# Attention's output bias: from an addition on GpSimd to a product with a row of ones on TensorE

## The chip, the cores and the metric

The kernel runs on one core of a Trainium2 chip. The metric is the device time of one execution in microseconds (us). Before the change its median is 1267.84 us over three runs (1267.67 to 1268.17).

## The reference

Two blocks of a small transformer, each an attention part and a mixture of experts, on x of 16 sequences x 256 tokens x 128 features, all in 32-bit floats. The change touches only the first part, attention with a selection of 32 keys for each query:

```python
# x is the layer norm of the residual rows here
Q, K, V = split(x @ w_qkv.T + b_qkv)            # Q and K are rotated (rope)
iq = (x @ w_iq.T + b_iq).reshape(B, S, 4, 64)   # index queries, 4 heads of 64
ik = x @ w_ik.T + b_ik
iw = x @ w_iw.T + b_iw                          # one weight for each index head
head_scores  = relu(einsum('bqhd,bkd->bhqk', iq, ik))
index_scores = einsum('bhqk,bqh->bqk', head_scores, iw)
# the 32 keys of highest index score stay, all others get -inf
attn = softmax(Q @ K.T / sqrt(128) + mask)
return (attn @ V) @ w_o.T + b_o                 # b_o: 128 numbers; added to the residual x
```

Since each row of `attn` sums to one, `attn @ (V @ w_o.T + ones * b_o)` is the same result as `(attn @ V) @ w_o.T + b_o`.

Behind it come a routed mixture of experts (8 experts, 2 for each token), a state-space part and a second mixture of experts. None of their code changes.

## The kernel before

The program is written by hand for each engine: TensorE (PE in the rows), VectorE (DVE), ScalarE (ACT), GpSimd (POOL) and SyncE (SP, it starts transfers). Each engine runs its own list in order, and semaphores order the engines. There is no planner; the order of work is the order in the source.

**Attention** (`attention`, lines 144 to 534) is a software pipeline over 16 sequences ("batches", s = 0 to 15), in 18 steps. In step s three batches are under work: the `front` of batch s, the `middle` of batch s - 1 and the `tail` of batch s - 2. Within a step each engine does, in this order:

- TensorE: transposes the normalised rows of batch s (L238, it waits for `iw_copied` of batch s - 1, which VectorE gives at L408); the products for Q and K (L245), index queries (L254), and index keys and V (L257); the logits of batch s - 1 (L269, it waits for `qk_sum`, GpSimd's rotated Q and K); V times w_o and the index weights of batch s (L276, L279), which it signals by `vo_ready`; the index scores of the first half of the queries (L296), the transposes of the probabilities of batch s - 2 (L304), the index scores of the second half (L296), and the product of probabilities and V times w_o (L316).
- ScalarE: copies the transposed rows (L343), exponentials of batch s - 2 (L347), copies with biases (L357, L361, L365), the copy of V times w_o into `VO` once `vo_ready` has come (L371), the normalised rows of batch s + 1 (L330), relu of the index scores, first half (L380), the copy of the transposed probabilities (L389), relu of the second half (L382, L383).
- VectorE: in step s it weights and adds the index scores of batch s - 1 (L419 for the first head, it waits for `relu_ready`; L422 for the other three), finds the 32 largest in four rounds of eight (L434, L438), updates the residual rows of batch s - 3 (L454, L460), takes the index weights of batch s out of PSUM (L408, it waits for `vo_copied`), and masks the logits of batch s - 1 (L442, L447, L450).
- GpSimd: adds the output bias to the residual rows of batch s (L517), multiplies Q and K by the rope table (L520, it waits for `rope_parts`, L357), adds the two parts (L525).

Some steps carry work of the next part, the dispatch of tokens to experts, beside this: a square root on ScalarE in steps 8 and 10 (L679) for which VectorE waits (L685), transposes and router products on TensorE in steps 10 and 11 (L716, L735), the choice of experts on VectorE in step 12, and from step 12 on four indirect DMAs for each step on GpSimd (L846) and scaling of the residual rows on ScalarE (L832). When all engines are through with attention, a barrier ends it. Then GpSimd issues the other 12 indirect DMAs of the first half of the tokens, and when these have landed, SyncE fetches the first tile of rows for the experts, which TensorE transposes at L1129.

The product of the change's line, before:

```python
for t in range(2):
    nc.tensor.matmul(b0[:, t * D:(t + 1) * D], IKV[v][:, S + t * P:S + (t + 1) * P],
                     w[:, 8 * P + IH:9 * P + IH], start=True, stop=True)
```

Each such product of 32-bit floats shows as two matmuls and two weight loads in the trace.

Of the kernel before, what the change touches and what calls it, by code (L numbers as in the profile page):

```python
# [12 lines left out]
ALU = mybir.AluOpType  # L13
# [3 lines left out]
B, S, D = 16, 256, 128  # L17
P = 128
T = B * S // P
TOPK = 32  # L20
IH, ID = 4, 64
# [8 lines left out]
ds = bass.ds  # L30
# [113 lines left out]
def attention(nc, rows, early, d, zeroed, X, shift, scales, ident, w, bias, b_iw, b_o, rope, loads, clear):  # L144
# [3 lines left out]
    with ExitStack() as ctx:  # L148
        m = Maker(nc, ctx, "at_")
        W2 = 2 * P  # L150
# [21 lines left out]
        b0, b12a, b12b, b3, b4 = bank  # L172
# [6 lines left out]
        xn_ready = m.sig("xn_ready", 2)  # L179
# [25 lines left out]
        x_updated = m.sig("x_updated", 2)  # L205


        b_added = m.sig("b_added")

        def steps(eng, step):  # L210

            step(0, 0, True, False, False)
            step(1, 1, True, True, False)
            for s in range(2, B):
                step(s, s % 4, True, True, True)
            step(B, 0, False, True, True)
            step(B + 1, 1, False, False, True)
# [4 lines left out]
        with nc.Block() as block:  # L222
            @block.sync
            def _(sp):
                loads(sp)

            @block.tensor
            def _(pe):
                def step(s, q, front, middle, tail):
# [42 lines left out]
                    if front:  # L272

                        pe.wait_ge(ikv_copied.sem, ikv_copied.after(s))
                        for t in range(2):
                            nc.tensor.matmul(b0[:, t * D:(t + 1) * D], IKV[v][:, S + t * P:S + (t + 1) * P],  # L276
                                             w[:, 8 * P + IH:9 * P + IH], start=True, stop=True)
                        for t in range(2):
                            ins = nc.tensor.matmul(b0[:, W2 + t * IH:W2 + (t + 1) * IH], xT[v][:, t * P:(t + 1) * P],  # L279
                                                   w[:, 8 * P:8 * P + IH], start=True, stop=True)  # L280
                        ins.then_inc(vo_ready.sem, 1)
                        pe.wait_ge(iq_copied.sem, iq_copied.after(s))
# [36 lines left out]
                    if s in TURN:  # L319
                        d.tensor_score(pe, TURN[s])  # L320

                steps(pe, step)

            @block.scalar
# [79 lines left out]
            def _(dve):  # L404
# [47 lines left out]
                def update(s, v):  # L452
                    dve.wait_ge(probs_ready.sem, probs_ready.after(s))
                    nc.vector.reciprocal(rinv[v][:], rsum[v][:]).then_inc(rinv_ready.sem, 1)  # L454
                    dve.wait_ge(rinv_ready.sem, rinv_ready.after(s))
                    dve.wait_ge(av_ready.sem, av_ready.after(s))
                    dve.wait_ge(b_added.sem, b_added.after(s))
                    for t in range(2):
                        x = X[:, ds(s * W2 + t * D, D)]
                        nc.vector.scalar_tensor_tensor(x, b4[:, t * D:(t + 1) * D], rinv[v][:, t:t + 1], x,  # L460
                                                       ALU.mult, ALU.add).then_inc(x_updated.sem, 1)
# [41 lines left out]

            @block.gpsimd
            def _(pool):
                clear()

                def step(s, q, front, middle, tail):
                    v = q % 2
                    if front:  # L510


                        pool.wait_ge(xn_ready.sem, xn_ready.after(s))
                        if s >= LAST:
                            pool.wait_ge(idx.sem, idx.after(s - 1))
                        x = X[:, ds(s * W2, W2)].rearrange("p (t d) -> p t d", d=D)
                        nc.gpsimd.tensor_tensor(x, x, b_o[:].unsqueeze(1).to_broadcast([P, 2, D]), ALU.add).then_inc(b_added.sem, 1)  # L517
                        pool.wait_ge(rope_parts.sem, rope_parts.after(s))
                        parts = RP[v][:].rearrange("p (r k s) -> p r k s", r=2, k=2)
                        nc.gpsimd.tensor_tensor(parts, parts, rope[:].rearrange("p (r s) -> p r s", r=2).unsqueeze(2).to_broadcast([P, 2, 2, S]),  # L520
                                                ALU.mult).then_inc(rotated.sem, 1)
                        pool.wait_ge(rotated.sem, rotated.after(s))
                        if not (isinstance(s, int) and s < 2):
                            pool.wait_ge(logits_ready.sem, logits_ready.after(s - 2))
                        nc.gpsimd.tensor_tensor(QK[v][:], RP[v][:, 0:2 * S], RP[v][:, 2 * S:4 * S], ALU.add).then_inc(qk_sum.sem, 1)  # L525
                    if s == LAST:
                        pool.wait_ge(zeroed.sem, zeroed.after(1))
                        d.pool_reweight(pool, 0, 0)
                    if LAST <= s < LAST + 4:
                        d.pool_scatter(pool, 0, HT // 4 * (s - LAST), HT // 4 * (s - LAST + 1), ALU.add)  # L530

                steps(pool, step)
                d.pool_reweight(pool, 0, 1)
                d.pool_scatter(pool, 1, 0, HT // 4, ALU.add)
# [1588 lines left out]
```

## Time and profile before

| | |
|---|---|
| median of three runs | 1267.84 us (1267.67 to 1268.17) |
| the profiled execution | 1262.61 us, its span 1260.8 us |
| TensorE busy / its weight loads | 989.4 us (78%) / 599.9 us (48%) |
| VectorE busy | 942.6 us (75%) |
| GpSimd busy | 837.2 us (66%) |
| ScalarE busy | 736.0 us (58%) |
| attention, from the start to its last instruction on VectorE | 232.46 us |

The span is the time between the first and the last instruction of the profiled execution; what lies around it is 1.8 us. All positions are in us from the start of the span. Shares of busy time are means over parts that different engines bound, so the argument is made from the attention part alone. In a timeline row the first number is the start, the second the time from the first to the end of the last of the merged instructions ("x4": four of them), then come engine, line, operation and output<-input; in brackets stands how long the engine had been idle before and who released it.

### The profile page before, as it was taken

The numbers are of one execution on the slowest core, as the hardware profiler recorded it, in microseconds if no ns is written. First come the engines' busy times: TensorE is split into PE (matmuls) and PEld (weight loads), VectorE is DVE, ScalarE is ACT, GpSimd is POOL, SyncE is SP. The second block draws the span as 40 slices with busy tenths as digits, with TensorE's granted clock in tenths as the row PEclk, the third lists the DMA queues.
The fourth block names the chain that finished last, engine by engine and source line by source line (L and its number), as shares of the span: only waits on it lengthen the run. The fifth ranks groups of instructions, "written<-read, shape, count | busy, mean of one in ns | idle before, by whom it ended". The sixth has DMA issues, their size and how long they took to land. (4 is left out here: it accounts for less than half of the span.)

```text
span 1260.8 us, 17033 instructions
## 1 busy us (share of the span) xinstructions
PE 989.4 (78%) x4202; PEld 599.9 (48%) x4202; DVE 942.6 (75%) x2310; ACT 736.0 (58%) x1636; POOL 837.2 (66%) x604
## 2 busy tenths in 40 slices
PE   5888867469999977888888888888876324989990
PEld 4666755348888832323242424333221223757770
DVE  6999899553333438899998989999998852757781
ACT  4767747255555568776666766867542213768750
POOL 3334248647437455989898987788966077747876
PEclk9998889579999989899989998989989656989995
DMA  9993012336535424444444443435442014746553
GB/s 272 177 162 129 1 10 22 30 49 93 82 68 94 81 41 122 132 145 136 144 135 141 138 146 127 137 133 169 146 149 89 1 46 76 121 88 123 114 103 65
DMA packets 140480, 133.50 MB, mean 106 GB/s; under 512 B 14578, under 2 KB 121698, under 8 KB 140258
## 3 DMA queue, kind: packets, MB, share of 16 engines
q1 hardware_dynamic: 107106, 115.55, 33.8%
q0 software_dynamic: 33280, 16.86, 11.9%
q8 instruction: 39, 0.64, 0.2%
q14 instruction: 55, 0.45, 0.1%
HBM read 98.66 MB, written 31.60 MB: 103 GB/s over the span
## 5 line engine op out<-in xcount | busy, mean ns | idle before, releaser
L1855 POOL TENSOR_TENSOR ss_HC<-ss_Hs,ss_Cb 128x512 f32<-128x512 f32 x256 | 325.2, 1367 | 83.0 <-PE ss_Y L1605 66.1
L1605 PE MATMUL ss_Y<-ss_HC,g_ident 128*128 128x512 f32 x512 | 270.9, 648 | 48.6 <-POOL ss_HC L1855 42.0
L1899 DVE TENSOR_TENSOR_SCAN ss_Hs<-ss_dA,ss_dBu 128x512 f32<-128x512 f32 x256 | 296.7, 1199 | 7.5 <-ACT ss_dA L1765 7.5
L846 POOL DMA_INDIRECT rows<-m_XS,g_slot x128 | 181.2, 1416 | 67.9 <-issue 35.8
L1765 ACT ACTIVATE ss_dA<-ss_delta,g_A 128x510 f32<-128x510 f32 x256 | 168.4, 712 | 74.2 <-DVE ss_Hs L1899 74.0
L1138 PE MATMUL m_x_UP<-g_m_w,m_x_gT 128*128 (+1 forms) x532 | 193.2, 469 | 0.0
L1605 PEld LDWEIGHTS ss_Y<-ss_HC,g_ident 128*128 128x128 f32 x512 | 92.1, 200 | 211.7 <-POOL ss_HC L1855 155.5
L1891 DVE TENSOR_TENSOR ss_dBu<-ss_duP,ss_Bb 128x512 f32<-128x512 f32 x256 | 162.8, 681 | 10.7 <-DMA ss_Bb<-bc_rows 9.1
L1158 PEld LDWEIGHTS m_x_DP<-g_m_w,m_x_hT 128*128 128x128 f32 x908 | 122.8, 191 | 61.7 <-issue 35.6
L1158 PE MATMUL m_x_DP<-g_m_w,m_x_hT 128*128 (+1 forms) x908 | 140.9, 285 | 2.4 <-ACT m_x_hT L1230 2.3
L1279 DVE SCALAR_TENSOR_TENSOR m_x_hid<-m_x_UP,m_x_G,m_x_sg 128x352 f32<-128x352 f32 x78 | 45.5, 583 | 116.4 <-ACT m_x_sg L1212 108.9
L1230 ACT ACTIVATE m_x_hT<-m_x_HP 128x256 f32<-128x256 f32 (+1 forms) x188 | 80.3, 427 | 87.1 <-PE m_x_HP L1148 55.4
L1118 POOL DMA_INDIRECT g_X<-out_rows,g_slot x64 | 99.6, 1557 | 37.9 <-issue 18.3
L520 POOL TENSOR_TENSOR at_RP<-at_RP,a_rope 128x1024 f32<-128x1024 f32 x16 | 39.6, 2475 | 90.9 <-ACT at_RP L357 90.9
L1138 PEld LDWEIGHTS m_x_UP<-g_m_w,m_x_gT 128*128 128x128 f32 x532 | 88.0, 194 | 18.1 <-issue 1.6
L1129 PE MATMUL m_x_TP<-g_ident,m_x_G 128*128 128x128 f32 x188 | 52.6, 280 | 38.4 <-DMA m_x_G<-rows 37.2
L1148 PE MATMUL m_x_HP<-g_ident,m_x_hid 128*128 128x128 f32 x454 | 80.6, 273 | 2.5 <-DVE m_x_hid L1279 2.5
L1286 DVE TENSOR_TENSOR m_x_sg<-m_x_UP,g_m_b 128x352 f32<-128x352 f32 x110 | 57.6, 524 | 33.0 <-PE m_x_UP L1138 24.7
L1106 POOL DMA_INDIRECT g_X<-out_rows,g_slot x32 | 49.3, 1540 | 44.3 <-DMA out_rows<-m_x_YO 32.8
L1570 PE MATMUL ss_Q<-ss_xpad,ss_w_conv 128*128 128x512 f32 x128 | 58.9, 605 | 5.8 <-ACT ss_xpad L1695 5.8
L1212 ACT ACTIVATE m_x_sg<-m_x_UP 128x352 f32<-128x352 f32 x78 | 36.2, 464 | 38.7 <-PE m_x_UP L1138 37.6
L1148 PEld LDWEIGHTS m_x_HP<-g_ident,m_x_hid 128*128 128x128 f32 x454 | 56.1, 142 | 4.0 <-DVE m_x_hid L1279 2.6
(271 smaller groups left out, 1746.7 us busy)
## 6 DMA issues: line engine op xcount, KB each, us to landing
ss_Bb<-bc_rows SPq DMA_DIRECT2D x64, 512.0 KB, 4.9
ss_Cb<-bc_rows SPq DMA_DIRECT2D x64, 512.0 KB
rows<-g_Z SPq DMA_DIRECT2D x2, 5031.0 KB, 49.1
m_x_G<-rows SPq DMA_DIRECT2D x156, 64.5 KB
out_rows<-m_x_YO SPq DMA_DIRECT2D x156, 64.0 KB
g_m_w<-in_w_up SPq DMA_DIRECT2D x1, 2816.0 KB, 10.7
g_m_b<-in_b SPq DMA_DIRECT2D x1, 2160.0 KB, 11.7
g_X<-in_x SPq DMA_DIRECT2D x4, 512.0 KB, 6.1
```

What stands on the lines that cost most here:

```text
L846: self.nc.gpsimd.indirect_dma_start(self.XG, bass.IndirectOffsetOnAxis(self.rt.slot[k][:, t:t + 1], 0), self.XS[:, t, :], None, compute_op ...
L1118: nc.gpsimd.indirect_dma_start(X[:, t * D:(t + 1) * D], None, Y[0:(h + 1) * NH * P, :], bass.IndirectOffsetOnAxis(rt.slot[k][:, t:t + 1], ...
L1138: ins = nc.tensor.matmul(UP[v % 2][:, at:at + n], gT[v % 2][:], w.w[:, ds(e + c, n)], start=True, stop=True)
L1148: ins = nc.tensor.transpose(HP[0:n, c * P:(c + 1) * P], hid[v % 2][:, c0:c0 + n], ident[:])
L1158: ins = nc.tensor.matmul(DP[v % 2][:, 0:D], hT[v % 2][0:n, c * P:(c + 1) * P], w.w[0:n, ds(e + WU + c * D, D)], start=c == 0, stop=c == NC ...
L1230: ins = nc.scalar.activation(hT[v % 2][:, 0:full], HP[:, 0:full], ACT.Copy)
L1570: ins = nc.tensor.matmul(dst, w_conv[:, h, k, :], xpad[:, h, :, k:k + S], start=k == 0, stop=k == K)
L1605: ins = nc.tensor.matmul(Yp[:, h, :], ident[:], HC[n % 2][:, h, :], start=False, stop=n == N - 1)
L1765: nc.scalar.activation(dA[n % NA][:, h, :, 1:S], seqs(delta[v][:, h, :])[:, :, 1:S], ACT.Exp, scale=A[:, h, n:n + 1]).then_inc(dA_ready.se ...
L1855: nc.gpsimd.tensor_tensor(HC[n % 2][:, h, :], Hs[n % 4][:, h, :], Cb[g % 2][:, n % 2, :], ALU.mult).then_inc(hc_ready.sem, 1)
L1891: v_.tensor_tensor(dBu[:, h, :], duP[:, h, :], Bb[g % 2][:, n % 2, :], ALU.mult).then_inc(dBu_ready.sem, 1)
L1899: v_.tensor_tensor_scan(Hs[n % 4][:, h, :], dA[n % NA][:, h, :, :].rearrange("p s t -> p (s t)"), dBu[:, h, :], 0.0, ALU.mult, ALU.add).th ...
```

## The change

The residual rows no longer get the bias from GpSimd. Instead TensorE adds it to the rows of V times w_o, as a product of a row of 128 ones (one partition high) with `b_o` (its first partition), accumulated into the same PSUM region. VectorE no longer waits for `b_added` in its update, and GpSimd no longer waits for the normalised rows. A memset of the row of ones on GpSimd is new, with a wait for it on TensorE in step 0.

```diff
-        b_added = m.sig("b_added")
+        row, row_set = m.sb("row", [1, P]), m.sem("row_set")
...
                         pe.wait_ge(ikv_copied.sem, ikv_copied.after(s))
+                        if s == 0:
+                            pe.wait_ge(row_set, 1)
                         for t in range(2):
                             nc.tensor.matmul(b0[:, t * D:(t + 1) * D], IKV[v][:, S + t * P:S + (t + 1) * P],
-                                             w[:, 8 * P + IH:9 * P + IH], start=True, stop=True)
+                                             w[:, 8 * P + IH:9 * P + IH], start=True, stop=False)
+                            nc.tensor.matmul(b0[:, t * D:(t + 1) * D], row[0:1, :], b_o[0:1, :], start=False, stop=True)
...
                     dve.wait_ge(av_ready.sem, av_ready.after(s))
-                    dve.wait_ge(b_added.sem, b_added.after(s))
...
             def _(pool):
+                nc.gpsimd.memset(row[:], 1.0).then_inc(row_set, 1)
                 clear()
...
-                        pool.wait_ge(xn_ready.sem, xn_ready.after(s))
                         if s >= LAST:
                             pool.wait_ge(idx.sem, idx.after(s - 1))
-                        x = X[:, ds(s * W2, W2)].rearrange("p (t d) -> p t d", d=D)
-                        nc.gpsimd.tensor_tensor(x, x, b_o[:].unsqueeze(1).to_broadcast([P, 2, D]), ALU.add).then_inc(b_added.sem, 1)
```

## Rows read from the trace of the kernel before

**Rows 1.** Busy time by stretch: span, PE, PEld, DVE, ACT, POOL, PEclk, DMA, GB/s

```profile
54.00:66.00 12.00, 11.00 (x70) 8.59 (x66) 11.90 (x50) 9.35 (x23) 4.36 (x3) 1.00 1.27 185
...
92.00:94.00 2.00, 2.00 (x6) 1.53 (x6) 2.00 (x7) 0.37 (x2) 0.00 (x0) 0.50 0.83 203
...
290.00:310.00 20.00, 20.00 (x123) 16.19 (x122) 6.58 (x18) 10.78 (x27) 14.75 (x12) 1.00 0.59 92
```

**Rows 2.** Groups of POOL, 0 to 235: busy, mean ns | idle before, releasers

```profile
L520 POOL TENSOR_TENSOR at_RP<-at_RP,a_rope 128x1024 f32<-128x1024 f32 x16 | 39.6, 2475 | 90.9 <-ACT at_RP L357 90.9
...
L517 POOL TENSOR_TENSOR g_X<-g_X,a_b_o 128x256 f32<-128x256 f32 x16 | 13.4, 835 | 7.1 <-DVE at_WK L422 5.7 <-ACT at_Xn L330 0.8
```

**Rows 3.** Timeline, TensorE around the changed product, step 15

```profile
210.79 0.52 PEld L276 LDWEIGHTS at_b<-a_w,at_IKV 128*128 128x128 f32 x4 [0.93 <-ACT at_IKV L365]
...
211.23 0.53 PEld L279 LDWEIGHTS at_b<-a_w,at_xT 128*128 128x128 f32 x4
...
211.77 1.13 PE L296 MATMUL at_SC<-at_IKV,at_IQ 64*128 64x256 f32 x8
```

**Rows 4.** Timeline, one round between ScalarE and TensorE, step 15

```profile
203.24 0.59 ACT L383 ACTIVATE at_R<-at_b 128x512 f32<-128x512 f32 x1
...
205.26 0.37 ACT L343 ACTIVATE at_xT<-at_b 128x256 f32<-128x256 f32 x1
...
205.68 1.99 PE L245 MATMUL at_b<-at_xT,a_w 128*128 128x256 f32 x8 [1.64 <-ACT at_xT L343]
...
211.88 0.38 ACT L371 ACTIVATE at_VO<-at_b 128x256 f32<-128x256 f32 x1 [1.14 <-PE at_b L279]
...
215.10 0.59 ACT L383 ACTIVATE at_R<-at_b 128x512 f32<-128x512 f32 x1
```

**Rows 5.** Timeline, the instructions before which VectorE waited for ScalarE

```profile
23.70 0.35 DVE L419 TENSOR_SCALAR at_WK<-at_R,at_IW 128x256 f32<-128x256 f32 x1 [0.55 <-ACT at_R L383]
...
112.22 0.25 DVE L685 RECIPROCAL m_d_sc<-m_d_t 128x16 f32<-128x16 f32 x1 [0.41 <-ACT m_d_t L679]
...
128.28 0.35 DVE L419 TENSOR_SCALAR at_WK<-at_R,at_IW 128x256 f32<-128x256 f32 x1 [1.28 <-ACT at_R L383]
...
140.06 0.25 DVE L685 RECIPROCAL m_d_sc<-m_d_t 128x16 f32<-128x16 f32 x1 [1.03 <-ACT m_d_t L679]
...
157.30 0.35 DVE L419 TENSOR_SCALAR at_WK<-at_R,at_IW 128x256 f32<-128x256 f32 x1 [1.21 <-ACT at_R L383]
```

**Rows 6.** Timeline, first weighting of batch 15 on VectorE

```profile
215.56 0.62 DVE L419 TENSOR_SCALAR at_WK<-at_R,at_IW 128x256 f32<-128x256 f32 x2
```

**Rows 7.** Timeline, first product of steps 3, 6 and 7 on TensorE

```profile
44.62 0.38 PE L238 MATMUL at_b<-g_ident,at_Xn 128*128 128x128 f32 x2
...
77.50 0.41 PE L238 MATMUL at_b<-g_ident,at_Xn 128*128 128x128 f32 x2 [0.36 <-DVE at_IW L408]
...
89.56 0.41 PE L238 MATMUL at_b<-g_ident,at_Xn 128*128 128x128 f32 x2 [1.18 <-DVE at_IW L408]
```

**Rows 8.** Timeline, VectorE's mask of steps 8, 14 and 15, GpSimd beside the last

```profile
100.61 0.43 DVE L442 TENSOR_SCALAR at_WK<-at_WK 128x512 f32<-128x512 f32 x1
...
201.64 1.09 DVE L442 TENSOR_SCALAR at_WK<-at_WK 128x512 f32<-128x512 f32 x1
...
213.08 1.27 POOL L525 TENSOR_TENSOR at_QK<-at_RP 128x512 f32<-128x512 f32 x1
213.16 1.48 DVE L442 TENSOR_SCALAR at_WK<-at_WK 128x512 f32<-128x512 f32 x1
```

**Rows 9.** Timeline, the Q and K products of steps 7 and 9

```profile
90.44 3.15 PE L245 MATMUL at_b<-at_xT,a_w 128*128 128x256 f32 x8 [0.47 <-ACT at_xT L343]
...
115.66 3.78 PE L245 MATMUL at_b<-at_xT,a_w 128*128 128x256 f32 x8 [1.37 <-ACT at_xT L343]
```

**Rows 10.** Timeline, end of attention and first expert tile

```profile
231.85 0.61 DVE L460 SCALAR_TENSOR_TENSOR g_X<-at_b,at_rinv,g_X 128x128 f32<-128x128 f32 x2 [3.83 <-PE at_b L316]
...
260.70 0.45 PE L1129 MATMUL m_x_TP<-g_ident,m_x_G 128*128 128x128 f32 x1 [8.65 <-DMA m_x_G<-rows]
```

## The prediction

> **What bounds the kernel now.** I read the busy time by stretch first. Inside attention VectorE is busy for 11.90 us of 12 in a plain stretch, and behind attention TensorE is busy for 20.00 of 20 while the expert tiles run [rows 1]. So the attention part has one length, set mostly by VectorE, and whatever moves its end moves all that follows: VectorE's last update at 231.85 lets the barrier go, GpSimd then issues its other twelve indirect DMAs, and the first expert tile at 260.70 has waited 8.65 us for rows that these bring [rows 10]. I take the shift of attention's end at full price for the whole time.
>
> Next I read who waits for whom up to 235 us. GpSimd's groups show that it is not the bound: before the rope product it idles for 90.9 us in total, waiting for ScalarE, and the bias addition that the change removes sits in front of that wait [rows 2]. What the reader is to look for instead is every place where VectorE waits for ScalarE, because there VectorE is not the bound and the round between TensorE and ScalarE is. There are five of weight: 0.55 us at 23.70, 0.41 at 112.22, 1.28 at 128.28, 1.03 at 140.06 and 1.21 at 157.30 [rows 5].
>
> Last I followed that round in a timeline. In step 15 it goes from the relu at 203.24 over the copy of transposed rows at 205.26, the Q and K products at 205.68 (TensorE had waited 1.64 us for that copy), further copies and products, the copy of V times w_o at 211.88, for which ScalarE waited 1.14 us on TensorE, to the next relu at 215.10: 11.86 us a round [rows 4]. The changed product lies on this round, between a copy that TensorE waited for (0.93 us) and a copy that ScalarE waits for [rows 3, 4]. Time put in there is not covered by either engine.
>
> **The change part by part.**
>
> *GpSimd loses 16 additions*, 13.4 us of its busy time at 0.835 us each [rows 2]. In steps 0 to 12 they only lengthen its wait for the rope parts: worth nothing. In steps 13 to 15 GpSimd has DMAs to issue and gets through earlier, by about 0.7 us for each step at most. Nobody waits for it at a signal there, but it shares something with VectorE: the mask takes 1.09 us at 201.64 and 1.48 us at 213.16, where GpSimd's addition from 213.08 to 214.35 runs beside it [rows 8]. The same instruction takes 0.43 us at 100.61, where GpSimd computes nothing beside it [rows 8]. So up to 0.66 + 1.05 = 1.7 us of VectorE's time can come back. I book it at nothing, because VectorE then only arrives earlier at the weighting of batches 14 and 15, and there it is barely behind ScalarE: the relu of batch 15 ends at 215.10 + 0.59 = 215.69, and of the two L419 instructions, 0.62 us together with one at 0.35, the second starts 0.27 us after the first, at 215.83 in batch 15 [rows 4 to 6]. That leaves 0.14 us (0.10 in batch 14, in the same way). If the round had room, the 1.7 us would be a gain; that is the lower bound of this part.
>
> The page GPSIMD Engine Reference of the Trainium skill, section Key points, says that GpSimd shares its SBUF interfaces with VectorE and contends with instructions in a two-port mode; the rows on the mask bear it out, and by that rule alone the change would gain the 1.7 us just named.
>
> *The wait for `b_added`* on VectorE and *the wait for the normalised rows* on GpSimd go: no idle time is laid to either in the list of waits, so nothing. *The memset of the row of ones* is one short instruction in front of three others on GpSimd, at 10.7 us, 9 us before TensorE needs it. It delays SyncE's weight transfers by as much, some 0.1 us (my estimate; the 128 x 256 addition that goes takes 0.835 us [rows 2]); the experts need these weights only after 130 us. Nothing. No DMA is added or moved.
>
> *TensorE gains* two products in each step, which show as four matmuls and four weight loads, since the product beside them does. Four of L276's take 0.44 us from start to the next line's start (210.79 to 211.23); four of L279's, with only 4 columns to stream, take 0.54 us (211.23 to 211.77) [rows 3]. The new ones have the shape of L276's apart from their height of one partition. No row shows that height. The nearest with fewer rows are the index scores on half the array: eight of 256 columns in 1.13 us [rows 3], against 1.99 us for eight of 256 columns on the full array [rows 4], about half. So the bounds for one step are 0.22 us (half of 0.44) and 0.54 us. I take d = 0.44 us: the gain of the half-height products comes from pairs that lie on different halves of the array, and here all four lie on the same partition.
>
> The Trainium skill's page TensorE: Matmul & The Clock Gate, section Why this matters for your kernels, states that a single product with 32 rows takes as long as one with 128. By that rule d is 0.44 us, by the half-height row 0.22; no run here shows which.
>
> *How d adds up on the end of attention.* I carry the lateness of TensorE's start of each step, with d = 0.44.
> - Batch 0: VectorE waits for the relu at 23.70 [rows 5], so VectorE is late by 0.44.
> - Step 2 starts when VectorE lets it (0.44). Step 3 starts at 44.62 without a wait, on TensorE's own time [rows 7]: 0.88; steps 4 and 5 likewise: 1.32, 1.76. Step 6 had waited 0.36: 1.76 + 0.44 - 0.36 = 1.84. Step 7 had waited 1.18: 1.84 + 0.44 - 1.18 = 1.10 [rows 7]. Step 8: 1.54. Whether VectorE feels it in batches 2 to 7 doesn't matter, since a wait there would be part of what is booked next.
> - Step 8, where VectorE waits for the root at 112.22: 1.54 + 0.44 = 1.98 late. The same at 128.28: 2.42; at 140.06: 2.86; at 157.30: 3.30 [rows 5].
> - Step 12 is long on VectorE alone, so the lateness stays 3.30. Batches 13, 14 and 15 run at the pace of the round: 3 x 0.44 = 1.32, less the 0.14 us of room in batch 15 [rows 4, 6]. Together 4.48 us.
>
> One thing in this sum is open: TensorE's clock. At 90.44 and 115.66 the eight Q and K products take 3.15 and 3.78 us [rows 9] against 1.99 [rows 4]; the granted clock is at 0.50 of full speed (1.2 GHz in place of 2.4) from 92 to 94, after TensorE had idled 1.18 and then 0.47 us in step 7 [rows 1, 7, 9]. With the lateness of 1.84 us the pause of 1.18 goes away. If the clock then holds, step 7 is shorter by 3.15 - 1.99 = 1.16 us and more in the next products, the lateness carried into step 8 is eaten, and only VectorE's own 0.44 stays: 0.44 + 6 x 0.44 - 0.14 = 2.94 us. No row tells which of the two comes; I take the middle, 3.7 us.
>
> **Sum.** The profiled execution took 1262.61 us, its span 1260.8 and 1.8 us around it, 5.2 us under the median of the runs, so a re-run of the same kernel can differ by as much as the sum that I make. Profiled: 1262.6 + 3.7 = 1266.3. Applied to the median: 1267.84 + 3.7 = **1271.5 us**. What a measurement can tell from no change is about 0.2%, 2.5 us.
>
> With d = 0.22 and the clock held: 0.22 + 6 x 0.22 - 0.14 = 1.4 us; with d = 0.54 and the clock as before: lateness 2.78 us in batch 8, then 6 x 0.54 - 0.14, 5.9 us. The likeliest case reaches from 1269.2 to 1273.7.
>
> **The rivals.**
> - *Hidden under VectorE (no change, 1267.8 us).* VectorE is busy 99% in plain steps [rows 1]. If the new products overlap with their neighbours, or the recovered 1.7 us of the masks [rows 8] balances a small d (d = 0.22 costs 1.4 us), nothing is left. Against it: VectorE's five waits, all on the round.
> - *The clock holds where it fell before (faster, 1264.7 us).* More work on TensorE could keep the granted clock up in steps 7, 9, 11 and 12. In step 9 that alone is 3.78 - 1.99 = 1.8 us on the Q and K products [rows 4, 9]. It can give VectorE no more than its waits, 1.28 + 1.03 + 1.21 = 3.5 us [rows 5], less 0.44 for batch 0: 3.1 us. It decides once step 9 runs at full clock, since it gains more than four times d. Against it: the fall at 115.66 comes after a wait of 1.37 us that depends on a table load of ScalarE and VectorE's scales, and the change leaves both. The Trainium skill's page TensorE: Matmul & The Clock Gate, section What's actually happening, says that the clock goes by how busy TensorE has been of late; the profile agrees so far that the low stretches come behind idle ones.
> - *The clock falls in more places (slower, 1275.1 us).* The shifted steps put the pauses of steps 14 to 16 elsewhere. In step 15 TensorE waits 1.64 us before the Q and K products and still has the full clock for them [rows 4], after a pause as long as the two of step 7 together. One fall costs 1.8 us in these products as at 115.66 [rows 4, 9], and about as much again in the products behind (my estimate, at the same ratio of 3.78 to 1.99): 3.6 us on top of 3.7.
> - *The change does not do what it says:* excluded by the diff; both products of a step run, the addition is gone.
>
> **How the numbers follow.** The round lengthened: 0.52. Hidden: 0.18. Clock held, faster: 0.13. Clock falls more: 0.17. Slower by over 0.2% (above 1270.4) is 0.17 and some 0.44 of the first case: 0.61. Within 0.2%: 0.18 + 0.08 = 0.26. Faster: 0.13. The range reaches from 1266 us, a part of the gain by the clock, to 1276 us, one further fall.
>
> **What would show it.** Right: the L276 line with twice as many instructions, L279 starting 0.9 us behind L276's start instead of 0.44; ScalarE's wait at L371 at 1.6 us instead of 1.14; VectorE's waits at L419 and L685 longer, new ones at batches 14 and 15; the mask at 0.4 to 0.6 us in steps 14 and 15; VectorE's last L460 2.9 to 4.5 us later than 231.85, and the first tile later by the same. Wrong: L371's wait longer by less than 0.3 us (d), an attention end that has not moved although the waits grew (cover that I missed), Q and K products at 1.99 us in steps 7 and 9 or at over 3 us elsewhere (the clock), or a difference that arises behind 260 us.

## The result: slower by 1.5%, five times the predicted loss

| kernel | median, us | lowest to highest | runs |
|---|---|---|---|
| before | 1267.76 | 1266.86 to 1268.17 | 4 |
| changed | 1286.20 | 1283.62 to 1287.28 | 4 |

The ratio is 1.0146, 95% interval 1.0132 to 1.0161: 18.4 us more, where 3.7 were predicted and 1276 us was the top of the range. The direction was right, the size was not. The profiled execution of the changed kernel took 1286.36 us, at its median; that of before took 1262.61 us, 5.2 below its own, so the two traces lie 23.7 us apart (spans 1284.5 and 1260.8) and some 5 of these are luck of that one execution of before.

Nearly all of it arises in attention. VectorE's last update starts 23.3 us later than at 231.85 [rows 10], the first expert tile 21.6 us later, with less waiting in front of it; the last 2.1 us between the two spans arise behind that tile. The timeline of the changed kernel:

```profile
255.17 0.61 DVE L462 SCALAR_TENSOR_TENSOR g_X<-at_b,at_rinv,g_X 128x128 f32<-128x128 f32 x2 [3.84 <-PE at_b L319]
...
282.30 0.45 PE L1129 MATMUL m_x_TP<-g_ident,m_x_G 128*128 128x128 f32 x1 [5.57 <-DMA m_x_G<-rows]
```

The changed product, step 4, TensorE's timeline (start, us, engine, line, operation; "x2" is one product, since each shows as two matmuls). In this kernel V's product is L278, the bias product L280, the index weights L282, the scores L299:

```profile
57.02 0.49 PE L278 MATMUL at_b<-a_w,at_IKV 128*128 128x128 f32 x2 [0.53 <-ACT at_IKV L368]
57.44 0.48 PE L280 MATMUL at_b<-a_b_o,at_row 1*128 1x128 f32 x2
57.85 0.49 PE L278 MATMUL at_b<-a_w,at_IKV 128*128 128x128 f32 x2
58.27 0.48 PE L280 MATMUL at_b<-a_b_o,at_row 1*128 1x128 f32 x2
58.68 0.61 PE L282 MATMUL at_b<-a_w,at_xT 128*128 128x4 f32 x4
59.22 1.55 PE L299 MATMUL at_SC<-at_IKV,at_IQ 64*128 64x256 f32 x8
60.70 1.11 PE L307 MATMUL at_b<-g_ident,at_PR 128*128 128x128 f32 x4
61.75 1.84 PE L299 MATMUL at_b<-at_IKV,at_IQ 64*128 64x256 f32 x8
```

The same place in the kernel before (there L276 is V's product, L279 the index weights, L296 the scores):

```profile
61.28 0.71 PE L276 MATMUL at_b<-a_w,at_IKV 128*128 128x128 f32 x4 [0.53 <-ACT at_IKV L365]
61.83 0.51 PE L279 MATMUL at_b<-a_w,at_xT 128*128 128x4 f32 x4
62.26 1.13 PE L296 MATMUL at_SC<-at_IKV,at_IQ 64*128 64x256 f32 x8
63.33 0.66 PE L304 MATMUL at_b<-g_ident,at_PR 128*128 128x128 f32 x4
63.91 1.13 PE L296 MATMUL at_b<-at_IKV,at_IQ 64*128 64x256 f32 x8
```

Read the starts, not the durations. From V's first product to the scores it was 62.26 - 61.28 = 0.98 us and is 59.22 - 57.02 = 2.20. So d, the price of the two bias products in one step, is 1.22 us, where I took 0.44 and bounded it at 0.54. The second thing to see is behind the group: the second scores take 1.84 us where they took 1.13. The granted clock says why (busy time by stretch; the third figure from the end is TensorE's granted clock as a share of 2.4 GHz):

```profile
50.00:52.00 2.00, 1.53 (x13) 1.24 (x11) 0.71 (x3) 1.62 (x4) 0.00 (x0) 1.00 1.28 148
...
60.00:62.00 2.00, 2.00 (x10) 1.02 (x10) 1.97 (x10) 1.64 (x4) 0.00 (x0) 0.50 1.26 186
62.00:64.00 2.00, 2.00 (x12) 1.42 (x13) 0.59 (x4) 0.82 (x2) 0.00 (x0) 0.70 1.24 164
```

It is at 1.2 GHz for a while in each of steps 2 to 5, where before it stood at 1.00 up to 90 us. In the stretch from 54 to 66 VectorE is busy for 9.76 us of 12, against 11.90 [rows 1]:

```profile
54.00:66.00 12.00, 11.00 (x57) 7.97 (x56) 9.76 (x42) 7.89 (x19) 3.62 (x2) 0.86 1.27 181
```

and its list of waits up to 245 us (total, times, longest) lays 23 waits of VectorE for ScalarE, 30.7 us together, to the four lines below. The same lines of the kernel before have 9 waits and 7.2 us in that list; [rows 5] shows the five that the prediction built on:

```profile
DVE at_WK L422 <- ACT at_R L386: 18.8, 12, 2.3
...
DVE m_d_sc L685 <- ACT m_d_t L679: 4.4, 2, 2.2
DVE at_WK L422 <- ACT at_R L383: 4.2, 5, 1.7
DVE at_IW L411 <- ACT at_VO L374: 3.3, 4, 1.8
```

### The profile page after: what moved, and what is told of

Read it like the earlier page. It is cut to its first block and busy times, and to the rows that moved or that the text cites. A ratio compares the mean times of both kernels' runs of the same rounds, so it can differ in the third digit from the quotient of the medians.

```text
span 1284.5 us, 17147 instructions
## 1 busy us (share of the span) xinstructions
PE 1019.8 (79%) x4266; PEld 618.0 (48%) x4266; DVE 943.1 (73%) x2310; ACT 736.0 (57%) x1636; POOL 824.8 (64%) x589
## 3 DMA queue, kind: packets, MB, share of 16 engines
q0 software_dynamic: 33280, 16.86, 11.7%
## 5 line engine op out<-in xcount | busy, mean ns | idle before, releaser
L1118 POOL DMA_INDIRECT g_X<-out_rows,g_slot x64 | 100.2, 1566 | 37.7 <-issue 18.6
## 6 DMA issues: line engine op xcount, KB each, us to landing
g_m_b<-in_b SPq DMA_DIRECT2D x1, 2160.0 KB, 11.4
```

The costliest lines, as they stand in the source:

```text
L1118: nc.gpsimd.indirect_dma_start(X[:, t * D:(t + 1) * D], None, Y[0:(h + 1) * NH * P, :], bass.IndirectOffsetOnAxis(rt.slot[k][:, t:t + 1], ...
```

## The experiments

Two theories stood after the result. **A**: what costs is the change of height. Between a product of 128 rows and one of 1 row lie 0.42 us from start to start, between two of 128 rows 0.22; four such changes in a step. **B**: the added products cost as such, or the half of the change on GpSimd does something that I didn't see (the rivals R1 to R3 of the expectations are forms of it). Below, "round" is the time from TensorE's logits product to that of the next step (steps 4 to 5 unless said), and d is taken as above, from V's first product to the scores. The kernels of one batch ran on one chip beside the kernel before, whose medians there were 1267.59, 1266.63 and 1266.63 us, with more scatter than in the first measurement (1260.39 to 1272.46 us in the first batch). Each ratio is the estimate of its batch with its 95% interval, and can differ by 0.2% from the ratio of two medians. A trace shows one execution: those of the grouped kernel, of the one product and of the 64 and 32 rows are the fastest of their four, that of the changed kernel's repetition is the slowest of its four.

**No bias at all.** GpSimd's addition is gone and nothing is in its place, so the bias is left out of the result.

```diff
-        b_added = m.sig("b_added")
...
-                    dve.wait_ge(b_added.sem, b_added.after(s))
...
-                        pool.wait_ge(xn_ready.sem, xn_ready.after(s))
...
-                        x = X[:, ds(s * W2, W2)].rearrange("p (t d) -> p t d", d=D)
-                        nc.gpsimd.tensor_tensor(x, x, b_o[:].unsqueeze(1).to_broadcast([P, 2, D]), ALU.add).then_inc(b_added.sem, 1)
```

> The GpSimd half of the change alone: its addition goes and no product comes in its place (the output bias is left out). Theory A, the loss of 18.4 us lies in TensorE's product alone: 1266 to 1268 us, with the masks of steps 14 and 15 near 0.43 us where they took 1.09 and 1.48 us. Rival R1, part of the loss comes from taking work off GpSimd (its operations now start elsewhere beside VectorE): above 1270 us.

Measured 1263.18 us, ratio 0.9976 (0.9943 to 1.0008): below the 1266 to 1268 us expected, and within the noise the time of before. The masks of steps 14 and 15 take 0.43 us, as expected, and attention ends only 0.3 us earlier (231.54 against 231.85). GpSimd's half of the change is worth nothing that can be measured, and costs nothing.

**The product alone.** The product of height 1 is added and GpSimd's addition kept; the bias is counted twice.

```diff
+        b_added.base = 1
+        row = m.sb("row", [1, P])
...
+                        if s == 0:
+                            pe.wait_ge(b_added.sem, 1)
...
-                                             w[:, 8 * P + IH:9 * P + IH], start=True, stop=True)
+                                             w[:, 8 * P + IH:9 * P + IH], start=True, stop=False)
+                            nc.tensor.matmul(b0[:, t * D:(t + 1) * D], row[0:1, :], b_o[0:1, :], start=False, stop=True)
...
+                nc.gpsimd.memset(row[:], 1.0).then_inc(b_added.sem, 1)
```

> The TensorE half alone: the product of height one is added and GpSimd keeps its addition (the output bias is counted twice). Theory A: as the changed kernel, 1283 to 1288 us, with 1.66 us from the first V product to the index weights' product where before it was 0.55. Rival R1: clearly below 1280 us.

Measured 1286.3 us, ratio 1.016 (1.0096 to 1.0225), the whole loss; d is 1.22 us here too. It is TensorE's half alone.

**Full height.** The stationary operand is 128 x 128 with 1/128 everywhere, and all 128 equal rows of the bias stream through: the same sum, and no change of height.

```diff
-        row, row_set = m.sb("row", [1, P]), m.sem("row_set")
+        row, row_set = m.sb("row", [P, P]), m.sem("row_set")
...
-                            nc.tensor.matmul(b0[:, t * D:(t + 1) * D], row[0:1, :], b_o[0:1, :], start=False, stop=True)
+                            nc.tensor.matmul(b0[:, t * D:(t + 1) * D], row[:], b_o[:], start=False, stop=True)
...
-                nc.gpsimd.memset(row[:], 1.0).then_inc(row_set, 1)
+                nc.gpsimd.memset(row[:], 1.0 / P).then_inc(row_set, 1)
```

> Same number and width of products, but 128 partitions high (128 x 128 of 1/128, times all 128 equal rows of b_o). Theory A, the price is the change of height between 128 and 1, some 0.2 us at each of four changes in a step: now d falls from 1.2 to the forecast 0.44 us, the clock no longer falls in steps 2 to 5, and the time is 1270 to 1273 us, what the prediction's sum gave. Rival R2, four more matmuls of any shape cost this much (the round was fuller than read): 1280 us or more.

Measured 1264.19 us, ratio 0.9993 (0.997 to 1.0015), faster than the 1270 to 1273 us expected. TensorE's timeline:

```profile
62.46 0.49 PE L278 MATMUL at_b<-a_w,at_IKV 128*128 128x128 f32 x2 [0.53 <-ACT at_IKV L368]
62.78 0.39 PE L280 MATMUL at_b<-a_b_o,at_row 128*128 128x128 f32 x2
63.01 0.39 PE L278 MATMUL at_b<-a_w,at_IKV 128*128 128x128 f32 x2
63.23 0.39 PE L280 MATMUL at_b<-a_b_o,at_row 128*128 128x128 f32 x2
63.45 0.51 PE L282 MATMUL at_b<-a_w,at_xT 128*128 128x4 f32 x4
63.89 1.13 PE L299 MATMUL at_SC<-at_IKV,at_IQ 64*128 64x256 f32 x8
```

128 times the arithmetic, the same number of products accumulated into the same region, and the loss is gone: 0.22 us from product to product, d = 63.89 - 62.46 - 0.98 = 0.45 us. The weight loads show what differs. Here the loads for the bias product start 0.11 us ahead of its matmul (62.67 against 62.78):

```profile
62.45 0.30 PEld L278 LDWEIGHTS at_b<-a_w,at_IKV 128*128 128x128 f32 x2 [0.93 <-ACT at_IKV L368]
62.67 0.30 PEld L280 LDWEIGHTS at_b<-a_b_o,at_row 128*128 128x128 f32 x2
```

In the changed kernel they don't run ahead (57.43 against 57.44):

```profile
57.02 0.30 PEld L278 LDWEIGHTS at_b<-a_w,at_IKV 128*128 128x128 f32 x2 [0.93 <-ACT at_IKV L368]
57.43 0.29 PEld L280 LDWEIGHTS at_b<-a_b_o,at_row 1*128 1x128 f32 x2
```

**Grouped: two changes of height in place of four.** First both products of V, then both of height 1.

```diff
                         for t in range(2):
                             nc.tensor.matmul(b0[:, t * D:(t + 1) * D], IKV[v][:, S + t * P:S + (t + 1) * P],
-                                             w[:, 8 * P + IH:9 * P + IH], start=True, stop=False)
-                            nc.tensor.matmul(b0[:, t * D:(t + 1) * D], row[0:1, :], b_o[0:1, :], start=False, stop=True)
+                                             w[:, 8 * P + IH:9 * P + IH], start=t == 0, stop=False)
+                        for t in range(2):
+                            nc.tensor.matmul(b0[:, t * D:(t + 1) * D], row[0:1, :], b_o[0:1, :], start=False, stop=t == 1)
```

> Height one, but both V products first and then both bias products, so two changes of height in a step and not four. Theory A: d = 4 x 0.11 + 2 x 0.2 = 0.84 us, and a time between the full-height kernel and the changed one, about 1276 to 1281 us. Rival R3, each product of height one is slow in itself, wherever it stands: as the changed kernel, 1283 us or more.

Measured 1281.02 us, ratio 1.0124 (1.0071 to 1.0178). Its four runs, 1275.12 to 1285.60 us, don't tell it from the changed kernel; the timeline does:

```profile
52.48 0.71 PE L278 MATMUL at_b<-a_w,at_IKV 128*128 128x128 f32 x4 [0.53 <-ACT at_IKV L369]
53.12 0.71 PE L281 MATMUL at_b<-a_b_o,at_row 1*128 1x128 f32 x4
53.76 0.61 PE L283 MATMUL at_b<-a_w,at_xT 128*128 128x4 f32 x4
54.30 1.13 PE L300 MATMUL at_SC<-at_IKV,at_IQ 64*128 64x256 f32 x8
```

d = 54.30 - 52.48 - 0.98 = 0.84 us. Against full height 0.39 us for two changes, 0.2 us each, as for the four of the changed kernel: (1.22 - 0.45) / 4 = 0.19.

**One product of height 1.** As grouped, but one product of 256 columns for both halves.

```diff
...
-                            nc.tensor.matmul(b0[:, t * D:(t + 1) * D], row[0:1, :], b_o[0:1, :], start=False, stop=True)
+                        nc.tensor.matmul(b0[:, 0:W2].rearrange("p (t d) -> p t d", d=D), row[0:1, :],
+                                         b_o[0:1, :].unsqueeze(1).to_broadcast([1, 2, D]), start=False, stop=True)
```

> The two products of V come first, and then one product of height 1 over both halves (256 columns) brings the bias: one change of height from 128 to 1 and one back, as in the grouped form, with one product of height 1 fewer. Theory A (each change of height between 128 and 1 costs about 0.2 us, whatever the number of products): the stretch from the first V product to the index weights is as in the grouped form, about 1.2 to 1.3 us, and the time about 1281 us, ratio 1.010 to 1.013. Theory B (each product of height 1 costs by itself): less than the grouped form by one product, and the time near 1275 us, ratio 1.006.

Measured 1281.23 us, ratio 1.0135 (1.009 to 1.0181); d = 0.82 us. Halving the number of products, at the same columns, changes nothing: two changes cost what they cost. Theory B's stretch, one product shorter than the grouped one, is out, and its 1275 us lies under each of the four runs (1276.42 to 1284.31).

**64 and 32 rows.** Is it height 1, or any height but 128? The ones are 1/64 on 64 partitions, then 1/32 on 32.

```diff
-        row, row_set = m.sb("row", [1, P]), m.sem("row_set")
+        row, row_set = m.sb("row", [64, P]), m.sem("row_set")
...
-                            nc.tensor.matmul(b0[:, t * D:(t + 1) * D], row[0:1, :], b_o[0:1, :], start=False, stop=True)
+                            nc.tensor.matmul(b0[:, t * D:(t + 1) * D], row[:], b_o[0:64, :], start=False, stop=True)
...
-                nc.gpsimd.memset(row[:], 1.0).then_inc(row_set, 1)
+                nc.gpsimd.memset(row[:], 1.0 / 64).then_inc(row_set, 1)
```

> The product of the change with 64 rows (a stationary operand of 1/64 on 64 partitions, 64 rows of the bias) where the change has 1 row; same order, same number of products. Theory A in its narrow form (height 1 is what costs): as with 128 rows, four products in 0.44 us more, time about 1264 to 1267 us, ratio 0.999 to 1.002. Theory A in its wide form (every change of height costs about 0.2 us): the stretch is 1.66 us as in the change, time 1283 to 1287 us, ratio 1.013 to 1.016. The index scores of height 64 follow products of height 128 in the kernel before with no gap of that size, so I expect the narrow form, or something between.

> The product of the change with 32 rows (stationary 1/32 on 32 partitions). Half height took exactly the stretch of height 1 (1.66 us from the first V product to the index weights) and lengthened the round from 10.69 to 11.91 us. Theory A in its wide form (every change of height costs about 0.2 us, whatever the height): again 1.66 us, rounds of 11.91 us where the clock is full, time 1279 to 1287 us, ratio 1.011 to 1.016. Theory C (the cost grows with the rows that are left out, and the agreement of 64 and 1 rows is an accident): another stretch than 1.66 us.

Measured for 64 rows 1281.56 us, ratio 1.014 (1.0092 to 1.0189), for 32 rows 1284.61 us, 1.0154 (1.0102 to 1.0205). I had leaned to the narrow form, and it was wrong. TensorE's timeline with 64 rows:

```profile
54.40 0.49 PE L278 MATMUL at_b<-a_w,at_IKV 128*128 128x128 f32 x2 [0.53 <-ACT at_IKV L368]
54.81 0.49 PE L280 MATMUL at_b<-a_b_o,at_row 64*128 64x128 f32 x2
55.23 0.49 PE L278 MATMUL at_b<-a_w,at_IKV 128*128 128x128 f32 x2
55.65 0.48 PE L280 MATMUL at_b<-a_b_o,at_row 64*128 64x128 f32 x2
56.06 0.61 PE L282 MATMUL at_b<-a_w,at_xT 128*128 128x4 f32 x4
56.60 1.13 PE L299 MATMUL at_SC<-at_IKV,at_IQ 64*128 64x256 f32 x8
```

The spacing is that of height 1 to 0.01 us, and with 32 rows too; d is 1.22 us for 64, 32 and 1 rows. Going from 128 rows to fewer and back is what costs, however many are left out. The scores behind the group take 1.13 us here: this execution has the lengthened stretch without the falls of the clock in steps 2 to 5.

**A change of height in TensorE's wait.** The kernel before, GpSimd's addition kept, with one more product per step, its result unread, issued where TensorE waits for the copies of IKV; once with 1 row, once with 128.

```diff
+                        pe.wait_ge(iq_copied.sem, iq_copied.after(s))
+                        nc.tensor.matmul(b3[:, 0:D], ident[0:1, :], b_o[0:1, :], start=True, stop=True)
                         pe.wait_ge(ikv_copied.sem, ikv_copied.after(s))
```

> The kernel before, GpSimd's addition kept, with one more product of height 1 in each step, whose result nobody reads: TensorE issues it after the logits, in its wait for the copies of IKV (0.53 us of idle time), so the two changes of height (about 0.3 us each) lie in that wait as far as it reaches. Theory A1 (the changes of height cost TensorE only the time in which nothing runs, and that time on the path is what is lost): V's products start at most 0.1 us later, the time is that of before within 2 us, ratio 0.999 to 1.002. Theory A2 (products of height 1 bring the granted clock down wherever they stand): the clock falls in steps 2 to 5 as in the changed kernel, although the round is hardly longer, and the time is 5 us or more above that of before.

> As the one with the product of height 1 in the wait, but with a product of 128 rows in its place: the difference between the two is that of height alone. Under each theory the time is that of before within 2 us (ratio 0.999 to 1.002) and the clock stays at 1.00 in steps 2 to 5; a time above that would say that an extra product in this place costs by itself, and then the one with the height 1 has to be read against this one.

Measured 1266.67 us, ratio 1.0007 (0.998 to 1.0033) with 1 row, and 1267.15 us, 1.0011 (0.9988 to 1.0034) with 128. The timeline of the first:

```profile
60.73 0.48 PE L275 MATMUL at_b<-a_b_o,g_ident 1*128 1x128 f32 x2
61.32 0.71 PE L278 MATMUL at_b<-a_w,at_IKV 128*128 128x128 f32 x4
...
62.30 1.14 PE L298 MATMUL at_SC<-at_IKV,at_IQ 64*128 64x256 f32 x8
```

V's product starts at 61.32, against 61.28 before. Two changes of height a step are free where TensorE would have idled, and the clock stays at 1.00 from 22 to 106 us. So in this execution products of low height didn't bring the clock down. The bias products themselves weren't put there: they write to the PSUM bank from which ScalarE is then still copying IKV, and no run shows what that would do.

This execution answers one more question. The clock did not fall in steps 7 and 9, where it falls before: the rounds that end there took 12.07 and 13.49 us against 13.74 and 16.33, and TensorE was 3.5 us ahead of before in step 9 (118.77 against 122.25). Step 12, which is long on VectorE, took it back; attention ended 0.3 us earlier.

**The same length without a change of height.** Three products of full height, each with a third of the bias, for each half.

```diff
-        row, row_set = m.sb("row", [1, P]), m.sem("row_set")
+        row, row_set = m.sb("row", [P, P]), m.sem("row_set")
...
-                            nc.tensor.matmul(b0[:, t * D:(t + 1) * D], row[0:1, :], b_o[0:1, :], start=False, stop=True)
+                            for k in range(3):
+                                nc.tensor.matmul(b0[:, t * D:(t + 1) * D], row[:], b_o[:], start=False, stop=k == 2)
...
-                nc.gpsimd.memset(row[:], 1.0).then_inc(row_set, 1)
+                nc.gpsimd.memset(row[:], 1.0 / (3 * P)).then_inc(row_set, 1)
```

> The bias as three products of height 128 for each half of V, each with a third of it (stationary 1/384): no change of height, but six products of 0.22 us, so the stretch from the first V product to the index weights should be 0.44 + 6 x 0.22 = 1.76 us, 0.1 us more than in the changed kernel. Theory D (only the length of the stretch counts: a round is 10.69 us plus what the stretch is longer by): rounds of 12.0 us in steps 3 to 5 where the clock is full, end of attention 16 to 18 us later than before, time 1280 to 1288 us, ratio 1.012 to 1.018. Theory A with a part of its own for the change of height beyond the stretch (the granted clock that falls in steps 2 to 5 of the changed kernel): no such falls here, rounds of 12.0 us all the same, time nearer 1278 to 1283 us, as with half height.

Measured 1277.73 us, ratio 1.0097 (1.0064 to 1.0129); d = 67.85 - 65.52 - 0.98 = 1.35 us. The round came out as foreseen, to 0.04 us:

```profile
51.92 1.03 PE L269 MATMUL at_LG<-at_QK 128*128 128x256 f32 x4
63.96 1.03 PE L269 MATMUL at_LG<-at_QK 128*128 128x256 f32 x4
76.00 1.03 PE L269 MATMUL at_LG<-at_QK 128*128 128x256 f32 x4
```

12.04 us a round, and no fall of the clock from 46 to 106 us. With a longer stretch than the changed kernel's it loses less than that kernel did in its own measurement (1.0132 to 1.0161), but the changed kernel repeated on this chip, below, gave 1.012 with an interval that overlaps. So length alone brings most of the loss: 0.97%, against 1.46% in the first measurement and 1.2% on this chip, with intervals too wide for a share. Theory D's 1280 to 1288 us was too high for it, and theory A's 1278 to 1283 us just so. Whether the rest belongs to the changes of height, beyond the time that they take, isn't shown.

**The changed kernel once more**, beside the last two.

> The changed kernel once more, on the chip of these runs, for a second profiled execution. If the granted clock falls in steps 2 to 5 belong to the change of height, rounds of 13.4 us are seen again in steps 2 to 5 and the attention ends 23 us later than before. If they differ from execution to execution, the rounds without a fall are of 11.91 us as with half height, and the end of attention lies anywhere from 16 us (no falls) to 23 us (four more falls) later; the time is then 1279 to 1287 us, ratio 1.012 to 1.016.

Measured 1281.97 us, ratio 1.012 (1.0072 to 1.0167). Its attention ends 23.2 us later than before, as in the first execution, but by another way. Round by round, TensorE's logits products of the first execution:

```profile
41.80 1.03 PE L269 MATMUL at_LG<-at_QK 128*128 128x256 f32 x4
55.46 1.03 PE L269 MATMUL at_LG<-at_QK 128*128 128x256 f32 x4
68.92 1.03 PE L269 MATMUL at_LG<-at_QK 128*128 128x256 f32 x4
82.38 1.03 PE L269 MATMUL at_LG<-at_QK 128*128 128x256 f32 x4
```

13.66, 13.46, 13.46 us. In the second: 13.61, then 11.91, 11.90, 11.91 us; it had lost 6.6 us already by step 1, in stretches at the lower clock:

```profile
22.00:26.00 4.00, 4.00 (x19) 3.39 (x20) 0.17 (x1) 1.62 (x4) 0.47 (x1) 0.56 1.14 329
26.00:30.00 4.00, 3.05 (x11) 1.74 (x10) 2.01 (x6) 2.01 (x5) 0.00 (x0) 0.50 1.22 254
```

So the second expectation holds: the falls are not in the same steps each time, the rounds without one are of 11.91 us, and that both executions end 23 us late lies at the end of what it allowed.

All profiled executions side by side. "Late" is the start of TensorE's logits product in that step, and of VectorE's last update, against the execution of before, in us; the last column is my prediction's own sum, 14 d - 1.68 with the clock as before. "Late" holds a difference of the start as well: V's first product, before any bias product has run, starts between 19.14 us (changed) and 20.79 (changed, again), at 20.51 with 64 and 20.29 with 32 rows, against 19.50 before.

| kernel | d | full-clock round | late, step 1 | step 8 | step 13 | last update | 14 d - 1.68 |
|---|---|---|---|---|---|---|---|
| before | 0 | 10.70 | 0 | 0 | 0 | 0 | |
| full height | 0.45 | 11.14 | 0.3 | -0.3 | 0.7 | 1.7 | 4.6 |
| one product of height 1 | 0.82 | 11.52 | 0.9 | 5.5 | 9.4 | 13.0 | 9.8 |
| grouped | 0.84 | 11.52 | 1.1 | 4.2 | 7.4 | 11.1 | 10.1 |
| 32 rows | 1.22 | 11.92 | 2.0 | 6.2 | 11.3 | 15.9 | 15.4 |
| 64 rows | 1.22 | 11.91 | 2.2 | 6.5 | 11.7 | 16.5 | 15.4 |
| product alone | 1.22 | 11.91 | 5.8 | 11.4 | 17.9 | 22.4 | 15.4 |
| changed, again | 1.22 | 11.91 | 6.6 | 12.1 | 18.6 | 23.2 | 15.4 |
| changed | 1.22 | 11.91 | 3.3 | 13.7 | 18.8 | 23.3 | 15.4 |
| longer, full height | 1.35 | 12.04 | 1.1 | 6.2 | 8.8 | 12.3 | 17.2 |

The third column is the cleanest reading of the study. For before it is the shortest of its rounds at full clock, in steps 2 to 6; the others go up to 11.24 us, with TensorE waiting for VectorE in step 6 [rows 7]. With the products a round takes 10.70 us plus d, to 0.02 us, in nine executions, in the rounds from step 3 to step 6 without a fall of the clock (in the changed kernel's first execution, from step 6 to step 8). So d is covered only as far as the rounds before were the longer ones, by up to 0.5 us: from step 2 to step 6 about half of it with full height (1.0 us more for four times 0.45), a fifth at d = 1.22 (64 rows: 4.1 us more for four times 1.22).

## Why the prediction was wrong, step by step

**The step that failed is the price of the two products, d.** "Four of L276's take 0.44 us [...] The new ones have the shape of L276's apart from their height of one partition. No row shows that height." I bounded d by 0.22 and 0.54 us; it was 1.22. By my own sum those 0.78 us more in each step are 10.9 of the 14.7 us that I was short. Both bounds came from products among their like, and neither contains what the change really adds, four switches between 128 rows and another height at 0.19 us each. I had set only the height against a row and not the order in which heights follow each other. The 0.44 itself was right for products of full height (0.45). The hint stood in the trace of before and I didn't look: the four matmuls of L304 lie between two groups of 64 rows and take 63.91 - 63.33 = 0.58 us from start to start, where four of L276's, the same shape among their like, took 0.44 [rows 3]; that is 0.14 us more. It is only the part of two switches that falls on this group. Matmul by matmul the scores on either side are stretched too: from the first pair of the second scores to the next pair it is 0.32 us, between the pairs behind 0.22, and as much is added on the other side. Together that is 0.35 us for two switches, 0.18 each. Four of them on top of 0.44 would have given 1.14 us and, by my own sum, 14.3 us of loss.

The upper bound of 0.54 held a part of a switch, and I read it as the price of four narrow products. The starts in [rows 3] are those of weight loads. The loads of L279 begin ahead of their matmul (211.23 against 211.34); those of the scores, with 64 rows, begin with theirs:

```profile
211.34 0.51 PE L279 MATMUL at_b<-a_w,at_xT 128*128 128x4 f32 x4
...
211.77 0.73 PEld L296 LDWEIGHTS at_SC<-at_IKV,at_IQ 64*128 64x128 f32 x8
```

From matmul to matmul L279's four take 0.43 us.

The Trainium skill's rule that I cited, that a product with 32 rows takes as long as one with 128, is right for the product (0.48 us with 32 rows, 0.49 with 128, both beside a switch) and said nothing on the neighbours. The rule that bears on them is on its page TensorEngine Tiling (Array Packing), section Key Properties: "Changing tiling mode (not just tile) drains the TensorE". The traces agree in what can be seen of it: 64, 32 and 1 rows cost the same, the cost goes by the number of switches, and the weight loads don't run ahead across one. The page speaks of tiling modes; that a plain product of fewer than 128 rows among products of 128 is such a change is my reading, and no run shows the drain itself. The runs show the price.

**How d adds up came out in the middle, in part by luck, and was off at both ends.** With d = 1.22 my sum gives 15.4 us; the executions with 64 and 32 rows gave 16.5 and 15.9, of which 1.0 and 0.8 us were there before the first bias product. With d = 0.45 it gives 4.6 (my clock-held variant 3.0), and full height gave 1.7; with d = 1.35 it gives 17.2, and the longer full height gave 12.3. In all four the fall of the clock in step 7 stayed away: the round that ends with the logits product of step 7 took 11.91, 11.91, 11.18 and 12.03 us against 13.74 before. I had priced that as one of two variants, and it is the one that came. So the sum with the clock as before met the 64 and 32 rows although one of its terms did not come, and the agreement confirms no single term. So even with a change that cost what I took it to cost, 3.7 us would have been too much, and the time no different from before (ratio 0.9993).

**The clock.** My rival "falls in more places" had 0.17, and one fall of 3.6 us as its price. In the changed kernel's profiled execution it came on top, at 1.5 us a fall: four rounds of 13.66, 13.46, 13.46 and 13.42 us against 12.12, 11.91, 11.92 and 11.92 with 64 rows, 6.1 us in all. Executions with the same d differ by 7.4 us in attention's end (15.9 to 23.3), and beside the start the granted clock is what the traces show to differ between them. The rival "the clock holds" was to be worth 3.1 us; in the execution with 1 row in the wait it held in steps 7 and 9, and brought 0.3. What makes it fall in one and not in another stays open. Stretches below full clock between 20 and 60 us appear in three executions, the changed kernel's two and that of the product alone, all with height 1 and d = 1.22. They appear in none with full height, in the wait, or with 64 or 32 rows at the same d. But the times of the 64 and 32 rows (ratios 1.014 and 1.0154) don't differ from the changed kernel's second measurement (1.012), and their traces are of their fastest executions, so I don't take the three for a rule of height 1.

**GpSimd's half** was booked at nothing, and is worth nothing (0.9976, 0.9943 to 1.0008). One reading on the way was wrong and harmless: I wrote that no idle time was laid to GpSimd's wait for the normalised rows, and [rows 2] lays 0.8 us to it. The masks did become fast, 0.41 and 0.42 us in steps 14 and 15 against 1.09 and 1.48 [rows 8], as that step said:

```profile
221.28 0.41 DVE L445 TENSOR_SCALAR at_WK<-at_WK 128x512 f32<-128x512 f32 x1
...
234.36 0.42 DVE L445 TENSOR_SCALAR at_WK<-at_WK 128x512 f32<-128x512 f32 x1
```

Those 1.7 us bring nothing, as without any bias: there the masks take 0.43 us too and attention ends 0.3 us earlier. That the round takes them back is what I had argued; the runs show only that they don't reach the end. Nor does it need the addition gone: with 1 row in the wait and the addition kept, the masks of steps 14 and 15 take 0.43 us as well.

**The signs to look for.** ScalarE's wait before the copy of V times w_o was to grow from 1.14 to 1.6 us; with full height it is 1.59, in the changed kernel 2.36. The end of attention was to be 2.9 to 4.5 us later, and is 23.3. That the loss would arise before 260 us, on the round and in VectorE's waits, was right.

**A better version.** None beats the kernel before by more than can be measured. Whoever wants the bias on TensorE takes the full height: it gives the same sum, and its time is that of before.

## What to carry to other kernels

Price an added product together with its neighbours: where it has another number of rows than the products before and behind, count the switches and not the arithmetic; filling the operand up to the full 128 rows can be cheaper than sending one. Look in the trace for a place where the same switch already happens and take its spacing from start to start. And when a product lies between a copy that TensorE waits for and a copy that waits for TensorE, book its price in full once for each round, less what another engine's longer round covers (here up to 0.5 us).

## What was not expected of the hardware

- A switch between 128 rows and 64, 32 or 1 rows in consecutive fp32 products of 128 columns costs about 0.19 us at a granted clock of 1.00 (2.4 GHz), the same for the three heights; products among their like follow each other at 0.22 us.
- A product with 128 times the multiplications (128 rows of 1/128 in place of one row of 1) was cheaper by 0.38 us, with no switch there and back.
- Two executions of one kernel reached the same end of attention (23.2 and 23.3 us late) with the clock falling in different steps, and executions of kernels with one and the same d spread over 7.4 us. In another the clock held in two steps where it had fallen, TensorE was 3.5 us ahead, and attention ended only 0.3 us earlier.
